# Plain fp32 for the first six products of the last stage of a graph kernel, with a scaled x that GpSimd splits in place

## What is computed

```python
d = 1 / sqrt(sum(A, -1));  lap_mul(A, x) = d * (A @ (d * x))
z = leaky_relu(lap_mul(A, x) @ W1 + b1, 0.1)
d2 = |z_i|^2 + |z_j|^2 - 2 z z^T             # 8192 x 8192
S = exp(-sqrt(max(d2, 0) + 1e-10) / 2), kept where it is among the 4 largest of its row
A2 = S + A
out = layernorm(x + lap_mul(A2, x) @ W2 + b2)
```

## Time and profile before

| | us |
|---|---|
| median of 3 runs (2684.04 to 2685.13) | 2685.08 |
| the profiled execution, whole | 2689.35 |
| its span, first to last instruction | 2687.5 |
| last stage: first matmul of the tail to the end of the span | 2247.2 to 2687.5 |
| PE, DVE, ACT, POOL busy over the span | 2462.7, 2319.7, 1607.3, 1204.2 |
| DMA over the span | 718.59 MB, 267 GB/s |

### The profile page before, as it was taken

How to read it: one execution, slowest core, us unless ns; L and a number is a source line. 1 busy time by engine, 2 the same in 40 slices (tenths; PEclk the granted TensorE clock), 3 DMA queues, 4 the chain that set the end, 5 groups by cost and what they waited for, 6 DMA issues and landing times.

```text
span 2687.5 us, 29160 instructions
## 1 busy us (share of the span) xinstructions
PE 2462.7 (92%) x9356; PEld 1714.1 (64%) x9356; DVE 2319.7 (86%) x1411; ACT 1607.3 (60%) x1905; POOL 1204.2 (45%) x987
## 2 busy tenths in 40 slices
PE   1467999999999999899999999999999998899997
PEld 0133444444577777577878787877878775576775
DVE  7998889977788887999999999989999877488886
ACT  0000000000377776899998999889898875477775
POOL 0000000000000000067788878778787895777773
PEclk9678999999999999999999999999999999999999
DMA  9999999997699881035555555546555568999995
GB/s 384 421 403 407 396 421 421 421 421 288 232 373 344 338 331 40 0 114 176 148 164 149 168 148 153 165 132 176 143 174 150 169 186 330 397 402 402 401 391 216
DMA packets 147949, 718.59 MB, mean 267 GB/s; under 512 B 19024, under 2 KB 26960, under 8 KB 86608
## 3 DMA queue, kind: packets, MB, share of 16 engines
q1 hardware_dynamic: 124384, 670.49, 66.4%
q0 software_dynamic: 18800, 37.77, 5.7%
q10 hardware_dynamic: 4608, 8.39, 0.8%
HBM read 680.40 MB, written 36.18 MB: 267 GB/s over the span
## 4 chain that ended last, share of the span: by engine, by line
PE 58%; ACT 10%; DVE 10%; issue 9%; DMA 9%; POOL 3%; SPq 0%; ACTq 0%; POOLq 0%; DVEq 0%
PE PS L770 18%; PE PS L869 5%; PE PS L871 5%; PE PS L870 5%; DMA ring<-at 4%; ACT R L1144 3%; PE PS L837 3%; PE PS L913 3%; PE PS L974 3%; PE PS L924 3%; PE PS L914 3%; DVE R L1626 2%; PE PS L833 2%; PE PS L834 2%; DMA cache<-at 2%
## 5 line engine op out<-in xcount | busy, mean ns | idle before, releaser
L1302 POOL TENSOR_TENSOR al<-ring,ah 128x1024 fp32r<-128x1024 f32 x264 | 643.4, 2438 | 180.7 <-ACT ah L1115 168.3
L1626 DVE MAX8 R<-R 128x8 f32<-128x8192 f32 x64 | 555.8, 8685 | 70.6 <-ACT R L1144 70.5
L1144 ACT ACTIVATE R<-PS 128x1024 f32<-128x1024 f32 x512 | 518.0, 1018 | 117.2 <-PE PS L877 85.9
L1629 DVE FIND_INDEX8 R<-R,R 128x8 uint32<-128x8192 f32 x64 | 555.8, 8685 | 0.3 <-issue 0.3
L1275 POOL CAST zst<-zh 128x128 fp32r<-128x128 f32 (+1 forms) x64 | 26.2, 409 | 1115.6 <-DVE zl L1561 812.5
L869 PE MATMUL PS<-zh,zst 128*128 128x512 f32 x1024 | 407.7, 398 | 28.3 <-ACT PS L1130 12.3
L871 PE MATMUL PS<-zh,zst 128*128 128x512 f32 x1024 | 401.4, 392 | 0.0
L870 PE MATMUL PS<-zl,zst 128*128 128x512 f32 x1024 | 400.9, 392 | 0.0
L1130 ACT ACTIVATE PS<-R 128x1024 f32<-128x1024 f32 x310 | 318.0, 1026 | 6.6
L1049 ACT ACTIVATE tiny<-rowsum 128x4 f32<-128x4 f32 x16 | 3.3, 205 | 483.3 <-DVE rowsum L1496 483.3
L770 PE MATMUL PS<-cache,R 128*128 128x512 f32 x584 | 264.0, 604 | 16.0 <-DMA cache<-at 10.6
(11 more groups left out here) (181 smaller groups left out, 4523.8 us busy)
## 6 DMA issues: line engine op xcount, KB each, us to landing
R<-at SPq DMA_DIRECT2D x152, 1024.0 KB, 13.0
ring<-at SPq DMA_DIRECT2D x148, 1024.0 KB, 9.4
ring<-at SPq DMA_DIRECT2D x264, 512.0 KB, 3.8
cache<-at SPq DMA_DIRECT2D x117, 1024.0 KB, 20.2
raw_sq<-at SPq DMA_DIRECT2D x21, 1024.0 KB, 12.7
raw_z<-at SPq DMA_DIRECT2D x20, 1024.0 KB, 13.2
raw_ring<-at SPq DMA_DIRECT2D x20, 1024.0 KB
acc_dram<-R POOLq DMA_DIRECT2D x78, 256.0 KB, 5.7
```

Of the source, the lines that this page charges most:

```text
L1144: act.activation(score[j % 2][:, c * EC:(c + 1) * EC].rearrange("p (b c) -> p b c", b=2), pair(first, j, c), ACT.Copy).then_inc(copied, 1)
L1302: pool.tensor_tensor(al[:, k % SPLIT], raw[k % RAW], ah[:, k % SPLIT].bitcast(F32), ALU.subtract)\
L1626: v.max(top[:, j], score[j % 2]).then_inc(dve3, 1)
L1629: v.max_index(place[:, j], top[:, j], score[j % 2]).then_inc(placed, 1)
```

## The change

- `plan_tail` opens with eight quads of row 9 instead of six, and the lights stand at one to three places of each heavy row instead of two, so that all are through by u = 86 (before u = 101). The last quads of all, from u = 102 on, are the same as before. `FIN_AT` stays.
- The quads (9, 0) to (9, 5), u = 0 to 5, are plain: `xsh` holds x of groups 0 to 2 in fp32, loaded from `xs_dram` (`load_xf`, 512 KB for a group) instead of the two halves (1024 KB).
- POOL, in place of the rests of two quads, makes the halves of these groups: a copy rounded to fp32r into `xsl` (the high part), and, once PE has read the two quads of a group, the rest in place in `xsh`. For later quads `high_tile` and `low_tile` swap the two for h < 6.
- ACT's rounds, DVE's rests and the last group's chain start with quad u = 6: `s_of_distances` and `root_of_sums` stand behind ACT's round of u = 7, and `last_near_sums` and `last_scale_of_rows` before DVE's rests of u = 7 and u = 8.
- `load_xs` of groups 4 to 6 comes two quads ahead on SP's queue instead of one (group 4 before quad 7).

```diff
-BY_POOL = 2
+OPEN_PLAIN = 6
-OPEN_T, SUM_AFTER, ACC_AT = 6, 4, (9, 20, 40)
+FIRST, OPEN_T, SUM_AFTER, ACC_AT = OPEN_PLAIN, OPEN_PLAIN + 2, 4, (9, 20, 40)
...
-            if h in (B // 3, 2 * B // 3) and lights:
+            if h in (B // 5, 7 * B // 15, 11 * B // 15) and lights:
...
-        plain = [h >= LAST for b, h in tail]
+        plain = [h >= LAST or (b == HB and h < OPEN_PLAIN) for b, h in tail]
...
+            def load_xf(g):
+                sp.dma_start(xsh[:, g * GT:(g + 1) * GT].bitcast(F32),
+                             xs_dram[g * GT * P:(g + 1) * GT * P].rearrange("(t p) d -> p t d", p=P))                  .then_inc(s_xf[g], 16)
...
             for g in range(2):
                 load_t(g)
                 sp.wait_ge(gram, NE * (T - 1) + g + 1)
-                load_xs(g)
+                load_xf(g)
             load_t(2)
             sp.wait_ge(gram, NE * T)
+            load_xf(2)
             load_t(3)
-            load_xs(2)
             load_t(4)
+            load_xs(OPEN_PLAIN * TB // GT)
...
-                for g in range(3, G - 1):
-                    if u == tail.index((HB, g * GT // TB)) - 1:
+                for g in (*range(OPEN_PLAIN * TB // GT + 1, G - 1),):
+                    if u == max(RAW_T, tail.index((HB, g * GT // TB)) - 2):
                         load_xs(g)
...
                 if plain[u]:
-                    pe.wait_ge(xg_ok, chain_of(G - 1, False))
+                    if h >= LAST:
+                        pe.wait_ge(xg_ok, chain_of(G - 1, False))
+                    else:
+                        pe.wait_ge(s_xf[h * TB // GT], 16)
...
-                if u == BY_POOL:
+                if u == FIRST + 1:
                     s_of_distances(G - 1)
-                if u == BY_POOL + 1:
                     root_of_sums(G - 1)
...
-            for u in range(BY_POOL):
-                pool.wait_ge(rnd_t, u + 1)
-                pool.tensor_tensor(al_t[u % 2][:, :, :], raw_t[u % RAW_T], ah_t[u % 2][:, :, :].bitcast(F32),
-                                   ALU.subtract).then_inc(al_pool, 1)
+            for g in range(OPEN_PLAIN * TB // GT):
+                tiles = slice(g * GT, (g + 1) * GT)
+                pool.wait_ge(s_xf[g], 16)
+                pool.wait_ge(gram, NE * T)
+                pool.tensor_copy(xsl[:, tiles], xsh[:, tiles].bitcast(F32)).then_inc(xf_high, 1)
+                pool.wait_ge(xf_high, g + 1)
+                pool.wait_ge(prod_t, tail.index((HB, (g + 1) * GT // TB - 1)) + 1)
+                pool.tensor_tensor(xsh[:, tiles], xsh[:, tiles].bitcast(F32), xsl[:, tiles].bitcast(F32),
+                                   ALU.subtract).then_inc(xf_split, 1)
...
-            for u in range(BY_POOL, len(tail)):
-                if u == BY_POOL + 1:
+            for u in range(FIRST, len(tail)):
+                if u == FIRST + 1:
                     last_near_sums(lk)
-                if u == BY_POOL + 2:
+                if u == FIRST + 2:
                     last_scale_of_rows(lk)
```

More of the change, by code:

```diff
@@ L289, in build, with high_tile @@
             raw_t.append(sb(name, [P, TB, BC], at=where)[:, :, :])
+        swapped = OPEN_PLAIN * TB
+        def high_tile(t):
+            return xsl[:, t] if t < swapped else xsh[:, t]
         def low_tile(t):
-            return xsl[:, t] if t < (G - 2) * GT else xsh[:, t + GT]
+            return xsh[:, t] if t < swapped else xsl[:, t] if t < (G - 2) * GT else xsh[:, t + GT]
         ah_t = [sb(f"ah_t{k}", [P, TB, BC], F32R, at=top_of["ring"] + k * SLOT * 4) for k in range(2)]
@@ L394, in build @@
         acc_seeded = sem("acc_seeded")
+        s_xf = [sem(f"s_xf{k}") for k in range(OPEN_PLAIN * TB // GT)]
+        xf_high = sem("xf_high")
+        xf_split = sem("xf_split")
         rnd_t = sem("rnd_t")
-        al_pool = sem("al_pool")
         al_dve = sem("al_dve")
@@ L524, in build @@
         n_heavy = [f + 1 - n_light[f] for f in range(B)]
-        plain = [h >= LAST for b, h in tail]
+        plain = [h >= LAST or (b == HB and h < OPEN_PLAIN) for b, h in tail]
+        assert not any(plain[FIRST:OPEN_T])
         halved = [u for u in range(len(tail)) if not plain[u]]
@@ L530, in wait_rest @@
         def wait_rest(eng, u, part_=RESTS - 1):
[L532 to L535, removed]
+            eng.wait_ge(al_dve, RESTS * place_of[u] + part_ + 1)
         def wait_halves_free(eng, u):
@@ L725, in _ @@
             sp.wait_ge(s_split, 32 * (G - 1))
+            sp.wait_ge(s_xg, 16 * (G - 1))
             sp.wait_ge(placed, T - 1)
@@ L970, in quad @@
                 if plain[u]:
-                    pe.wait_ge(xg_ok, chain_of(G - 1, False))
+                    if h >= LAST:
+                        pe.wait_ge(xg_ok, chain_of(G - 1, False))
+                    else:
+                        pe.wait_ge(s_xf[h * TB // GT], 16)
                     pe.wait_ge(ld_t[u % RAW_T], 16 * (u // RAW_T + 1))
                     for k in range(TB):
-                        i = pe.matmul(bank, xg[:, (h * TB + k) % GT], raw_t[u % RAW_T][:, k],
+                        t = h * TB + k
+                        rows = xg[:, t % GT] if h >= LAST else xsh[:, t].bitcast(F32)
+                        i = pe.matmul(bank, rows, raw_t[u % RAW_T][:, k],
                                       start=from_zero and k == 0, stop=last and k == TB - 1,
@@ L978, in quad @@
                     return
-                pe.wait_ge(s_xs[h * TB // GT], 32)
+                if h < OPEN_PLAIN:
+                    pe.wait_ge(xf_split, h * TB // GT + 1)
+                else:
+                    pe.wait_ge(s_xs[h * TB // GT], 32)
                 n = place_of[u]
@@ L983, in quad @@
                     t = h * TB + k
-                    pe.matmul(bank, xsh[:, t], ah_t[n % 2][:, k], start=from_zero and k == 0, stop=False,
+                    pe.matmul(bank, high_tile(t), ah_t[n % 2][:, k], start=from_zero and k == 0, stop=False,
                               skip_group_check=True)
@@ L989, in quad @@
                         wait_rest(pe, u, k * RESTS // TB)
-                    i = pe.matmul(bank, xsh[:, h * TB + k], al_t[n % 2][:, k], start=False, stop=False,
+                    i = pe.matmul(bank, high_tile(h * TB + k), al_t[n % 2][:, k], start=False, stop=False,
                                   skip_group_check=True)
```

## The result

| | before | changed |
|---|---|---|
| median, us (7 runs each) | 2685.13 (2681.89 to 2687.92) | 2694.92 (2692.01 to 2700.65) |
| ratio | | 1.0036, 95% interval 1.0027 to 1.0046 |
| span of the profiled execution | 2687.5 | 2693.4 |

The spans differ by less than the medians.

The account below looks back on a forecast made before the run. It took POOL's gapless chain of gathers to bound the end: 8.6 us later scaled x plus 0.5 for small rows, all else 0, gave 9.1 on 2685.1, so 2694.2 us; range 2686 to 2700.

Parts of the forecast that it names:

- That the late gathers set the end: Last stage: POOL's chain of 256 gathers has no gap, and what moves its start moves the end.
- Quad 7's landing: Opening of the last stage: 11.75 units in the full DMA queue, 30.6 us, land it at 2271.1; small rows add 0.5.
- From there to the scaled x: Chain on ACT and DVE from quad 7's landing at 2271.1 to the end of the scaling at 2280.4.
- The store's landing: POOL's store of the last group: gathers begin 9.2 us after its issue ends; queue as full as now, 0 added.
- The start of the gathers: POOL's first gather: later by 8.6 us plus 0.5 for small rows, 9.1 us in sum.
- The pace of the gathers: POOL's time per gather beside a busier DVE: bounds 0 and 0.6 us slower, taken as 0.
- The denser lights at 0: Quads shifted before u = 102, ahead of ACT's last two waits for gathers: 0 us at the end.
- The quads' side of the opening: Opening: 1.5 units less loaded, 3.9 us of DMA; nothing of it reaches the end, since quads wait for gathers.
- POOL's splitting costs nothing: POOL ahead of its store: splitting done by about 2271, covered by the wait for the scaled x, 0 us.
- A: Rival: quads set the end, which goes by data, 3.9 us less, 2681.2 us; chance 0.10.
- B: Rival: the gathers start only 3 to 5 us later because quad 7 lands before its turn, 2689 us; chance 0.15.
- C: Rival: delays add up and ACT's clock falls, 3.0 us, plus 0.6 for the gathers' pace, 2698 us; chance 0.15.

Follow-up runs that it names:

- e4: The kernel before, with POOL writing zeros to an unread buffer 16 times between its store's landing and its first gather; 2692.9 us, ratio 1.0029.
- e6: The changed kernel with two gathers a tile instead of four; 2681.9 us, ratio to before 0.9982.
- e7: The kernel before, run once more unchanged for a second profile; span 2684.1 us.
- e3: The kernel before with only the denser lights of the change; 2690.5 us, ratio 1.0019.
- e10: The kernel before with the denser lights and two gathers a tile instead of four; 2689.6 us, ratio 1.0011.
- e11: The changed kernel with two gathers a tile and the lights two a row again from row 12 on; 2676.8 us, ratio to before 0.9968.
- e5: The kernel before with two gathers a tile instead of four; 2680.3 us, ratio 0.9979.
- e1: The changed kernel with the last group's chain on ACT and DVE ahead of quads 6 and 7 again; 2690.2 us, ratio to before 1.0015.
- e2: As e1, with POOL's splitting in place behind its store of the last group; 2689.2 us, ratio to before 1.0016.
- e8: As e1, with POOL's splits of groups 1 and 2 behind its store and lights two a row from row 12 on; 2685.2 us, ratio to before 0.9998.
- e9: As e8, with the three rounded copies of POOL's splitting moved ahead of its store; 2682.3 us, ratio to before 0.9988.

## Why the prediction was right, and where it was not

The forecast was 2694.2 us, +9.1; measured were 2694.9, +9.8. By its steps:

- **That the late gathers set the end** held: 32.3 us of waits at ACT, the same 60.8 us from the third wait to the end, e4 for the mechanism alone (7.8 us), e6 for its removal (13.0 us back). But the forecast took the kernel before to be bound by gathers outright; e7 shows it nearly level. That made no difference for this sum, since a later chain passes a level one at once.
- **Quad 7's landing** was the mis-sized term. Expected at 2271.1, 27.3 us behind the copy of that execution, it came at 2272.82, 30.0 us behind its own: 2.7 us late. The count of units holds only if the three fp32 groups cost more than their size. They are rows of 512 bytes, for which I took 0.5 us between bounds of 0 and 4; the trace of after leaves 2.7, inside the bounds. The DMA windows bear that out in part. They are 15 us long, from 2.8 us ahead of the copy to 12.2 behind it, of the changed kernel and then of before (columns as in the earlier trace rows):

```profile
2240.00:2255.00 15.00, 11.39 (x26) 5.55 (x27) 10.85 (x3) 1.51 (x2) 2.89 (x4) 0.89 1.04 350
```

```profile
2241.00:2256.00 15.00, 8.38 (x27) 6.17 (x28) 10.90 (x3) 6.52 (x5) 10.28 (x4) 0.89 1.02 395
```

The DMA engines have no gap in the changed kernel on average (share 1.04) and still move 45 GB/s less, 0.68 MB in these 15 us, which is 1.7 of the 2.7 us at 402 GB/s. The small rows were not measured alone.

- **From there to the scaled x**: expected 9.3 us, measured 9.1 (2272.82 to 2281.92). The store's landing took 8.8 instead of 9.2.
- **The start of the gathers** is so 10.6 us later than in the first profile of before (49.2 - 38.6) and 11.7 later than in the second, in place of 9.1.
- **The pace of the gathers** was taken as unchanged, with at most 0.6 us to the bad. It went to the good: 363.4 us for the 256, 2.2 to 3.9 less, so that the last gather stood at 2654.45 and not at about 2658. 11.7 - 2.2 = 9.5 us, 10.6 - 3.9 = 6.7 us against the first profile. Two errors of 2 to 3 us cancelled; that the sum came within 0.7 us is in that part luck.
- **The denser lights at 0** was wrong as an entry and right only under the limit: alone they cost 5 us (e3), and 5 to 9 with the gathers out of the way (e10). The step that failed is "ahead of the last two waits: also 0": I asked where quads move, and not what their row of split ones asks of DVE. The sum survived because the late gathers covered it: the same quads with half the gathers (e6) end 13.5 us earlier behind the copy.
- **The quads' side of the opening**, 3.9 us of data less, fits in size: 3.5 us (e11 against e5), only just clear of the scatter.
- **POOL's splitting costs nothing** held for the end, since `xg_ok` was later anyway (its last subtraction ends at 2271.6, 10.6 us before the store). It isn't free in itself: it blocked DVE for 2.9 us here, under ACT's longer wait, and for 3.9 us in e1, where nothing hides it.

Of the rivals, A (quads set the end, 2681) describes e6, not the changed kernel. B needed quad 7 to land before its turn; it landed 2.7 us after it. C's price, a fall of the clock behind the last wait, did not come: from the third wait on both kernels take 60.8 us.

What stays open: why the gathers' pace differs by up to 7 us between these kernels (361.4 in e3, 368.5 in e1); where the last 1.0 of quad 7's 2.7 us comes from; and why plain quads far apart cost what e3 and e10 show, for which the sum of DVE's work is an account and not a test. The last column of the table is 37.9 to 38.0 in every kernel but e3: the gathers set the end in all of these, and in e3 the quads did.

## What to carry to other kernels

Before a chain of small operations is moved "a few quads later", count what then stands ahead of it in its engine's row and what that waits for: here two roundings that waited for DMA pushed a root of 0.2 us by 11 us, and with it 256 gathers that had next to no slack. When several limits are level, an edit can hide its own losses and gains under one of them; run its parts with that limit removed (half the gathers) as well as alone. And where one engine's work is uneven between kinds of steps, look at the mix along the whole stretch, not only on average.

## What the runs showed of the hardware

**POOL and DVE block each other for whole instructions.** In the changed kernel DVE's first operation on the distances, 128 x 32 elements, took 2.35 us; in the same place it took 0.18 in the kernels without POOL's work there (before, e2, e8, e9). It ended at 2264.07, when POOL's subtraction of 2261.69 + 2.35 = 2264.04 ended; the next one took 0.95 while POOL's copy ran to 2265.02. DVE's search for the places of a whole row (FIND_INDEX8) beside POOL's first subtraction did not change (8.68 us, and 8.69 in e2, where POOL stood still). In e2 and e8 the same cost both sides: POOL's subtraction 3.2 instead of 2.35 us, its copy 2.0 instead of 1.0, and DVE's two halves of a rest 3.5 to 5.3 instead of 2.35. The Trainium skill (SBUF — State Buffer, "two separate sides") states an exclusive lock on a shared pair of ports, held for a whole instruction. It names as DVE's side operations with two SBUF inputs or in a two-port mode. The runs agree with the lock; the 2.35 us operation has one tensor as its input, as has the one of 2.13 us in e1, and whether they ran in such a mode the trace doesn't tell.

**SP's issues can take microseconds.** A DMA is issued in 0.3 to 0.5 us as a rule. In the changed kernel's opening some took up to 4.4 us, beginning beside the loads in rows of 512 bytes (`xsh<-xs_dram`); in the kernels that load the halves instead, the longest there took 2.5 us (e5):

```profile
2236.25 0.34 SPq L723 DMA_DIRECT2D R<-at  x1
...
2238.76 1.49 SPq L726 DMA_DIRECT2D xsh<-xs_dram  x1
2240.30 3.60 SPq L723 DMA_DIRECT2D R<-at  x1
...
2244.80 3.25 SPq L723 DMA_DIRECT2D raw_sq<-at  x1
```

While SP stands there, the loads behind it are issued later. Over 2240 to 2255 the DMA engines had work all the same (mean share 1.04), so the 1.7 us lost there are not theirs standing empty.
